# Token mixing of an attention and RWKV-FFN block: half of the scale instructions move from ScalarE to VectorE

## What is computed

```python
x = x + _layernorm(attn(_layernorm(x), Wq, bq, Wk, bk, Wv, bv))
x = x + _layernorm(ffn(_layernorm(x), W_r, W_k, W_v, mu_r, mu_k))

def ffn(x, W_r, W_k, W_v, mu_r, mu_k):
    x_prev = jnp.concatenate([jnp.zeros((B, 1, C), x.dtype), x[:, :-1, :]], axis=1)
    xr = mu_r * x + (1.0 - mu_r) * x_prev
    xk = mu_k * x + (1.0 - mu_k) * x_prev
    r = jax.nn.sigmoid(jnp.einsum('btc,dc->btd', xr, W_r))
    k = jnp.einsum('btc,dc->btd', xk, W_k)
    k_act = jnp.square(jax.nn.relu(k))
    return r * jnp.einsum('btc,dc->btd', k_act, W_v)
```

## Time and profile before

| | us |
|---|---|
| timed runs (two) | 5474.19 and 5525.55, median 5499.87 |
| profiled execution | 5321.89 |
| its span, slowest core (core 7) | 5320.3 |
| its span, fastest core (core 0) | 5276.5 |

### The profile page before, as it was taken

How to read it: one execution, slowest core, us unless ns; L and a number is a source line. 1 busy time by engine, 2 the same in 40 slices (tenths; PEclk the granted TensorE clock), 3 DMA queues, 4 the chain that set the end, 5 groups by cost and what they waited for, 6 DMA issues and landing times.

```text
span 5320.3 us, 51576 instructions; the slowest of 8 cores (5276.5 to 5320.3 us)
## 1 busy us (share of the span) xinstructions
PE 3204.1 (60%) x15744; PEld 1312.2 (25%) x15744; DVE 1792.2 (34%) x3726; ACT 2176.6 (41%) x3017; POOL 23.8 (0%) x32
## 2 busy tenths in 40 slices
PE   2976666186197666518529766652843976664283
PEld 1432222032142222213214222211321422221131
DVE  3112233543511232353351132336244023323625
ACT  3135544441514555443141445445324154454523
POOL 0000000000000000000000000000000000000000
PEclk9876666588597666658859766655975976665597
DMA  4110000302510000021341000002133100001213
GB/s 103 28 21 1 1 1 9 111 16 47 183 32 16 1 1 1 19 100 20 70 156 32 17 1 1 1 28 91 32 87 127 32 16 1 1 1 40 79 32 111
DMA packets 76272, 221.52 MB, mean 42 GB/s; under 512 B 10465, under 2 KB 10465, under 8 KB 76002
## 3 DMA queue, kind: packets, MB, share of 16 engines
q1 hardware_dynamic: 50978, 167.88, 9.2%
q0 software_dynamic: 25024, 50.33, 5.7%
HBM read 201.41 MB, written 67.11 MB: 50 GB/s over the span
## 4 chain that ended last, share of the span: by engine, by line
PE 43%; DVE 25%; ACT 18%; issue 8%; DMA 3%; DVEq 1%; SPq 1%; ACTq 1%
ACT S L464 13%; PE psA L509 9%; PE psA L305 8%; PE psB L305 8%; DVE S L588 6%; PE psB L452 5%; DVE S L561 3%; DVE S L739 2%; PE psA L347 2%; PE psA L802 2%; PE psB L802 2%; DMA out<-POOL 2%; PE psB L347 2%; DVE S L485 1%; DVE S L702 1%
## 5 line engine op out<-in xcount | busy, mean ns | idle before, releaser
L509 PE MATMUL psA<-S 128*65 128x512 bf16 (+4 forms) x3328 | 1004.1, 397 | 265.7 <-ACT S L464 170.0
L464 ACT ACTIVATE S<-psB 128x1024 bf16<-128x1024 f32 x896 | 916.7, 1023 | 349.5 <-PE psB L452 296.1
L452 PE MATMUL psB<-S 64*128 64x512 bf16 (+3 forms) x2560 | 590.6, 458 | 395.6 <-DVE S L588 386.5
L485 DVE TENSOR_TENSOR S<-S,CB 128x128 bf16<-128x128 bf16 x1024 | 230.8, 225 | 1351.5 <-ACT S L473 1040.0
L305 PE MATMUL psA<-S,W 128*128 128x512 bf16 x2048 | 503.1, 405 | 100.4 <-DVE S L744 53.1
L509 PEld LDWEIGHTS psA<-S 128*65 128x65 bf16 x3328 | 321.6, 135 | 788.2 <-issue 780.8
L305 PE MATMUL psB<-S,W 128*128 128x512 bf16 x2048 | 469.4, 389 | 0.0
L469 ACT ACTIVATE S<-psB 128x128 bf16<-128x128 f32 (+2 forms) x384 | 147.3, 384 | 772.9 <-PE psB L452 760.7
L225 ACT ACTIVATE S<-S 128x1024 bf16<-128x1024 bf16 (+1 forms) x192 | 202.9, 1057 | 470.4 <-DVE S L825 370.1
L561 DVE CAST S<-psA 65x2048 bf16<-65x2048 f32 x64 | 146.4, 2287 | 645.0 <-PE psA L509 610.9
L452 PEld LDWEIGHTS psB<-S 64*128 64x128 bf16 x2560 | 133.4, 98 | 852.0 <-issue 836.8
(11 more groups left out here) (97 smaller groups left out, 2788.2 us busy)
## 6 DMA issues: line engine op xcount, KB each, us to landing
S<-x SPq DMA_DIRECT2D x96, 512.0 KB, 4.1
POOL<-x SPq DMA_DIRECT2D x32, 512.0 KB, 5.4
yscr<-POOL SPq DMA_DIRECT2D x32, 512.0 KB, 2.6
yscr<-S SPq DMA_DIRECT2D x32, 512.0 KB, 2.9
POOL<-yscr SPq DMA_DIRECT2D x32, 512.0 KB, 6.2
S<-yscr SPq DMA_DIRECT2D x32, 512.0 KB, 6.0
out<-POOL SPq DMA_DIRECT2D x32, 512.0 KB, 4.5
out<-S SPq DMA_DIRECT2D x32, 512.0 KB, 4.0
```

The source lines that it names most:

```text
L452: blk["tS"] = E("tensor", lambda e, slot=slot, ki=ki, c0=c0, c1=c1, ch=ch, rb=rb: e.matmul(psB[:, 512 * slot:512 * slot + (c1 - c0)], S3[r ...
L464: t_exp = E("scalar", lambda e, slotA=slotA, half=half: e.activation(PT(half)[:, 0:1024], psB[:, 512 * slotA:512 * slotA + 1024], AF.Exp, ...
L485: tm = E("vector", lambda e, half=half, c0=c0, dlo=dlo, e2=e2: e.tensor_tensor(PT(half)[:, 512 * e2 + dlo - c0:512 * e2 + dlo - c0 + 128], ...
L509: last_pv = E("tensor", lambda e, ki=ki, h=h, e2=e2, cs=cs, ce=ce, half=half, c0=c0, fb=fb, lb=lb, qlo=qlo: e.matmul(psA[0:65, QW * e2 + ( ...
```

## The change

In the xk half of the mixing the scale instruction is issued on VectorE and no longer on ScalarE. The xr half keeps it on ScalarE. In both halves it takes 2047 columns, which are those that the mix reads, and not 2048. The chunks, the scratch halves and the tokens stay as they are.

```diff
-                    ttmp = E("scalar", lambda e, lo=lo, omcol=omcol, cc=cc, tmp=tmp: e.activation(
-                        tmp[:, 0:S], S1[:, lo:lo + S], AF.Identity,
-                        scale=CONST[:, omcol + cc:omcol + cc + 1]),
-                        waits=w, inc="A")
+                    if dst is S2:
+                        ttmp = E("scalar", lambda e, lo=lo, omcol=omcol, cc=cc, tmp=tmp: e.activation(
+                            tmp[:, 0:S - 1], S1[:, lo:lo + S - 1], AF.Identity,
+                            scale=CONST[:, omcol + cc:omcol + cc + 1]),
+                            waits=w, inc="A")
+                    else:
+                        ttmp = E("vector", lambda e, lo=lo, mucol=mucol, cc=cc, tmp=tmp: e.tensor_scalar(
+                            tmp[:, 0:S - 1], S1[:, lo:lo + S - 1],
+                            CONST[:, omcol + cc:omcol + cc + 1], None, ALU.mult),
+                            waits=w, inc="V")
```

## The result

| | before | with the change |
|---|---|---|
| all runs, median | 5307.83 us (13 runs) | 5313.55 us (14 runs) |
| lowest run | 5296.15 us | 5244.43 us |
| ratio | 1 | 0.9915, 95% interval 0.9893 to 0.9937 |
| profiled execution, span of its slowest core | 5320.3 us | 5242.9 us |

By their times the two runs of before that were known at the time of the prediction, 5474.19 and 5525.55 us, are not undisturbed (their clocks are not on record). With 13 runs the level of before turns out to be 5296 to 5308 us.

The account below looks back on a forecast made before the run. No engine fills the span; TensorE waits for a tanh queued behind ScalarE's scale instructions. Removing 47.2 us idle and 7.2 us slow clock takes 54.4 us from the 5499.87 us median: 5445.5 us, range 5420 to 5471, wide 5255 to 5525.

Parts of the forecast that it names:

- the sum: Token mixing and r projection: idle time removed plus slow-clock excess removed, 47.2 + 7.2 = 54.4 us gained.
- The case of a lower level: Whole kernel: its time level may lie 178 us below the known median, as in the profiled execution, giving 5267 us.
- the idle time: r projection: TensorE's wait for the tanh of block 0 goes entirely, 47.2 us over four sequences.
- the low clock behind it: r projection, block 2: its excess over 6.91 us after the idle stretch goes, 7.2 us over four sequences.
- The missing term: Rest of r, k and the FFN: follows at TensorE's pace and moves forward as a whole, no loss counted.
- Part 2, the cost: xk mixing: eight added VectorE instructions per sequence, estimated 1.41 us each, cost nothing, with 17 us to spare.
- rival C: Start of k: VectorE becomes late if an added instruction exceeds 3.55 us; 5476 us at 4.5 us; chance 0.02.
- Part 3: xr scale instruction on ScalarE: 2047 columns instead of 2048, about 1 ns, worth nothing.
- Hand-over: r projection: block 0's tanh starts when TensorE ends the block, psA free 4.8 us before block 1 ends.
- Rival A: r and k projections: TensorE's clock falls, blocks take 8.40 us, costing 83.4 us; 5529 us; chance 0.07.
- Rival B: Whole kernel: differences between cores and between timings blur the gain, so the slowest core shows nothing; 5500 us; chance 0.09.
- rival D: r projection: something else holds the tanh of block 0, so nothing is gained; 5500 us; chance 0.02.

Follow-up runs that it names:

- e2: The changed kernel, but the tanh of block 0 also waits until the fifth xk chunk is mixed on VectorE; ratio to before 1.001.
- e3: The kernel before, with only the columns of all 16 scale instructions cut from 2048 to 2047; ratio 0.9982.
- e1: The kernel before, all 16 scale instructions still on ScalarE, the xk ones queued in pairs behind the tanh evictions of blocks 0 to 3; ratio 0.9906.
- e9: The changed kernel once more, unaltered, as a yardstick; ratio to before 0.9887.
- e11: The changed kernel, but the tanh of block 0 waits for all eight xk chunks; its undisturbed execution took 5342.14 us.
- e10: The changed kernel with a zeroed scratch column, no first-column instruction and the mix split into tensor_scalar and bf16 tensor_tensor; ratio to before 0.9838.
- e5: The changed kernel with each added VectorE instruction issued four times; ratio to before 0.9872.
- e6: The changed kernel with each added VectorE instruction issued seven times; ratio to before 1.0042.
- e4: The changed kernel with the xr scale instructions on VectorE as well, none on ScalarE; ratio to before 0.990.
- e7: The changed kernel without the first-column instruction: scratch column 0 zeroed once a sequence, one mix over 2048 columns; ratio to before 0.9854.

## Why the prediction was right and where it was wrong

**The step that failed** is the one that carried the sum to the level of the time: "I take the same 54.4 us from the median: 5445.5 us". The median of 5499.87 us was not the level of the kernel; the 13 runs show it at 5296 to 5308 us, and the two that were known stand 166 us and more above that. The trace in hand said so in part: its own execution took 5321.89 us, and even it had cores 4, 5 and 7 at 0.710 to 0.713 beside others at 0.715 to 0.719. With a level of 5297 us the same sum gives 5243, and undisturbed executions came out at 5244 to 5258, 5250 on the mean. What failed is the reading of which execution is typical. The case of a lower level stood in the text, but only as an end of the range (5267, with 5255 as the limit) and not as the likelier one, although the only execution with clocks to look at pointed there.

**The sum was right in its two terms, and one was missing.** 54.4 us of 5300 is a ratio of 0.9897, inside the interval of 0.9893 to 0.9937, near its end; 45 us is the measured middle, and undisturbed runs beside one another give 46 to 50 us. Both terms are shown: the idle time (47.2 us) went to 0 and came back with the wait in e2 (46.3); the low clock behind it went from 8.22 us to 6.91 in block 2 and came back in e2 (7.7 us in all). That it was the clock stands in the traces: on core 7 before, PEclk was 0.50 from 1111.46 to 1113.00 us, where two weight loads in a row lie 0.43 us apart, 0.84 over block 2 and 1.00 in block 3; with the change (core 1) it is 1.00 in block 2, and in block 1, behind the short pieces of block 0 (PEclk 0.50), still 0.85. The 7.2 us are core 7's; on the other seven cores of that trace the excess of block 2 is some 8 to 10 us.

The missing term is what the prediction put at nothing: "What remains of r (six blocks), k and the FFN follows at TensorE's pace and moves forward as a whole". For r and k that holds (on core 0 the blocks from 3 of r to the last of k take 90 us a sequence, before and after). The last FFN projection became slower. On core 0, the four stretches from the end of k to the first statistic of the output (ScalarE, L225), as length, TensorE's busy time, PEclk and the DMA columns, before:

```profile
1177.78:1273.15 95.37, 67.20 (x385) 0.95 0.06 19
2488.59:2584.28 95.69, 67.14 (x385) 0.95 0.06 20
3803.54:3901.81 98.27, 70.10 (x385) 0.92 0.06 19
5114.62:5212.67 98.05, 69.88 (x385) 0.92 0.05 19
```

And with the change:

```profile
1165.20:1263.28 98.08, 69.91 (x384) 0.92 0.06 19
2469.34:2567.24 97.90, 69.72 (x384) 0.92 0.05 19
3772.72:3871.58 98.86, 70.06 (x384) 0.92 0.06 19
5077.22:5175.04 97.82, 69.65 (x384) 0.92 0.05 18
```

The four add up to 387.4 and 392.7 us. Over all eight cores the mean is 387.8 before and 385.8 in e3, which has the old wait; 393.0 with the change, 393.0 in e1 and 394.7 in e9, which have none; and 383.7 in e11, whose wait is twice as long. In e2, which has the old wait again, it is 386.4 without cores 4 and 5, whose clock in the last sequence was 0.76 and 0.75. The mean PEclk of the same stretches is 0.935 before, 0.941 in e3, 0.947 in e11 and 0.939 in those six cores of e2, and 0.919 with the change, 0.919 in e1 and 0.915 in e9. So in these seven traces, where TensorE has not idled ahead of block 2, its granted clock in the last FFN projection is lower, and that takes back 5 to 9 of the 54.4 us. (In e10, also without the wait, it is 0.929, with 390.3 us.) Why it is lower there, no run settles.

**Part 2, the cost.** The estimate of 1.41 us was mis-sized: the instruction takes 0.755 us. The nearest row had an fp32 input (0.813 us for 1024 columns), and scaling it by columns did not carry over to a bf16 one. By the measured time xk is ready 5.2 us earlier than by the estimate. It changed nothing, since e5 shows that even 3.3 us per chunk is covered: 22 us were to spare and not 17. The limit of 3.55 us per instruction, worked out for rival C, fits e5 and e6: 3.3 us is free, 5.9 us costs 19.4 us a sequence, and 8 x (5.9 - 3.55) is 18.8.

**Part 3** is nothing, as said (e3). **Hand-over:** "the tanh of block 0 can then start when TensorE has ended the block" holds (1062.91), and "nothing new waits behind it" holds too: of L305's two waits for another engine only the one for the xr chunks is left.

**Rival A** (the clock takes it back) came in small and in another place: not as blocks of 8.40 us through r and k, but as the 5 to 9 us of the last FFN projection. The pace of 8.40 us itself was seen, for something else: it is why the two traces differ by 78 and not 54 us (PEclk 0.81 at that pace, on core 7 from 190 to 310 us and on core 4 in the earlier trace rows, and 1.00 at 6.91 us). Executions with one die at a lower clock occur with both kernels; one of before, of 5493.45 us, had cores 4 to 7 at 0.678 to 0.682 beside 0.717 and 0.718. In the highest one with the change (5557.49 us), cores 0 to 3 ended between 5456.6 and 5556.0 at clocks of 0.665 to 0.675, and cores 4 to 7, in the same execution, between 5237.8 and 5249.1 at 0.715 to 0.718, which is where all cores end in an undisturbed one. What sets off the slower die was not tried and stays open; that it comes when cores of a die run dense matmuls at one time was a supposition of the rival, and no run tests it. Two readings of the prediction were too smooth here: on core 7 block 1 was slow as well as block 2 (8.22 us in the first sequence), and the rival has the pace of 8.40 us take the cores of a die together, where in the first K and Q projections of the trace before cores 6 and 7 have 0.81 and cores 4 and 5 have 0.93 and 0.95 (190 to 320 us, each from its own start).

**Rival B** (blurred) is what the medians of all runs show, 5307.83 and 5313.55 us. It does not hold for undisturbed runs: with the change they lie within 14 us of each other, and 46 to 50 us are plain. Rival C is ruled out because L305 has no new wait at the start of k (that comes only with e6), and rival D because the wait for the tanh is gone.

## What to carry to other kernels

In these traces an engine runs its queue in order: with all 16 scale instructions ahead of the tanh TensorE idled 11.8 us a sequence for it, with eight ahead not at all. So an instruction that another engine waits for should stand ahead of work that nobody needs yet; look for a wait that is far longer than the instruction waited for. Moving it in the queue (e1) gives the same as moving the work to another engine, and before adding work to an engine, work out its slack: here 22 us a sequence, with none in the xr half (e4). And read the level of a time from more than two executions, core by core, before subtracting from it.

## What was not expected of the hardware

A mix as one scalar_tensor_tensor over 2047 bf16 columns takes 2.35 us; the same as tensor_scalar (0.75 us) and tensor_tensor (1.23 us), both over 2048 bf16 columns in SBUF, takes 1.98 us, and 2.19 with gaps. The fused instruction was slower than its two halves. The odd start column is not the reason: in e7 it takes 2048 columns from column 0 and has 2.35 us as well.

Idle time removed in one stage went with a lower granted clock of TensorE in a later one: 0.92 and not 0.95 in the last FFN projection of two of core 0's four sequences, which starts about 100 us behind the place of the gap.
